# The last feed-forward layer as one stage: normalisation, router, dense experts and store

## Reference

```python
x = x + tanh(g_ffn[3]) * ffn(layernorm(x))
# ffn, H = 128, E = 16 experts of width 64, one shared expert of width 128
shared = (silu(x @ shared_gate_w) * (x @ shared_up_w)) @ shared_down_w
probs = softmax(x @ router_w)
topk_probs, topk_idx = top_k(probs, 2)
coeff = einsum('tk,tke->te', topk_probs, one_hot(topk_idx, E))
for e in range(E):
    routed += (silu(x @ gate_w[e]) * (x @ up_w[e])) @ down_w[e] * coeff[:, e]
return routed + shared
```

## Time and profile before

| what | us |
|---|---|
| median of three executions (2179.49 to 2183.73) | 2183.63 |
| the profiled execution | 2188.82 |
| its span | 2187.1 |
| last addition of the last attention ends | 2037.7 |
| normalisation ends | 2049.6 |
| router's logits on DVE | 2058.5 |
| last addition of the experts ends | 2181.4 |
| span ends, after the store | 2187.1 |

### The profile page before, as it was taken

How to read it: one execution, slowest core, us unless ns; L and a number is a source line. 1 busy time by engine, 2 the same in 40 slices (tenths; PEclk the granted TensorE clock), 3 DMA queues, 4 the chain that set the end, 5 groups by cost and what they waited for, 6 DMA issues and landing times. The chain is left out here.

```text
span 2187.1 us, 56100 instructions
## 1 busy us (share of the span) xinstructions
PE 1781.5 (81%) x22264; PEld 1239.0 (57%) x22265; DVE 1377.1 (63%) x2794; ACT 1248.9 (57%) x1585; POOL 1056.0 (48%) x1000
## 2 busy tenths in 40 slices
PE   1699636999938579999999999999627749999497
PEld 1244325888826436666666666666426638888354
DVE  3767376888854366555555655654425468888598
ACT  2357324787734236777777777777325537877221
POOL 1100004555641347777777777778442335555210
PEclk9779758999959869999999999999758869999699
DMA  6401100000041110000000000000221010000000
GB/s 172 79 6 11 26 0 1 3 3 3 2 134 40 32 36 13 12 10 13 12 10 12 12 11 12 12 11 7 64 78 44 22 40 3 3 3 3 10 15 28
DMA packets 95469, 55.15 MB, mean 25 GB/s; under 512 B 43549, under 2 KB 88936, under 8 KB 95126
## 3 DMA queue, kind: packets, MB, share of 16 engines
q1 hardware_dynamic: 87028, 42.61, 8.1%
q0 software_dynamic: 3584, 6.36, 0.8%
q10 hardware_dynamic: 4610, 2.71, 0.5%
HBM read 30.16 MB, written 13.75 MB: 20 GB/s over the span
## 5 line engine op out<-in xcount | busy, mean ns | idle before, releaser
L1412 POOL TENSOR_TENSOR aw_p_lo<-aw_p,aw_p_hi 128x512 f16<-128x512 f32 x512 | 576.8, 1158 | 190.5 <-issue 168.3
L1428 DVE TENSOR_REDUCE aw_max_part<-ps 128x1 f32<-128x512 f32 x512 | 351.3, 690 | 289.4 <-PE ps L1234 284.5
L851 POOL TENSOR_TENSOR ap_p_lo<-ap_p,ap_p_hi 128x512 f16<-128x512 f32 x256 | 291.0, 1158 | 206.2 <-issue 193.2
L1364 ACT ACTIVATE aw_p<-ps 128x1024 f32<-128x1024 f32 x256 | 259.9, 1015 | 206.1 <-PE ps L1265 204.0
L1279 PE MATMUL ps<-ctx_hi_lo,aw_p_hi 128*128 128x97 f16 x2048 | 288.7, 206 | 2.5 <-POOL aw_p_lo L1412 2.5
L1281 PE MATMUL ps<-ctx_hi_lo,aw_p_hi 128*128 128x96 f16 x2048 | 287.9, 207 | 0.0
L1283 PE MATMUL ps<-ctx_hi_lo,aw_p_lo 128*128 128x97 f16 x2048 | 287.3, 204 | 0.0
L1371 ACT ACTIVATE aw_p_hi<-aw_p 128x1024 f16<-128x1024 f32 x256 | 270.6, 1057 | 8.1
L1281 PEld LDWEIGHTS ps<-ctx_hi_lo,aw_p_hi 128*128 128x128 f16 x2048 | 197.7, 97 | 25.2
L1279 PEld LDWEIGHTS ps<-ctx_hi_lo,aw_p_hi 128*128 128x128 f16 x2048 | 196.3, 96 | 12.1 <-POOL aw_p_lo L1412 4.7
L1283 PEld LDWEIGHTS ps<-ctx_hi_lo,aw_p_lo 128*128 128x128 f16 x2048 | 201.7, 98 | 0.0
(11 more groups left out here) (422 smaller groups left out, 4874.3 us busy)
## 6 DMA issues: line engine op xcount, KB each, us to landing
sf_weights_raw<-in_L_w SPq DMA_DIRECT2D x24, 256.0 KB, 4.4
slot_scratch<-at_empty_rows SPq DMA_DIRECT2D x16, 260.0 KB
sf_fetched<-slot_scratch SPq DMA_DIRECT2D x16, 260.0 KB, 2.9
sf_weights_raw<-in_L_w SPq DMA_DIRECT2D x8, 512.0 KB
x_norm<-result_scratch SPq DMA_DIRECT2D x8, 256.0 KB, 4.0
aw_queries<-aw_queries SPq DMA_DIRECT2D x32, 64.0 KB, 1.9
aw_queries<-aw_q_lo SPq DMA_DIRECT2D x32, 64.0 KB, 2.0
raw<-in_L_q SPq DMA_DIRECT2D x3, 512.0 KB, 12.7
```

The costliest lines, as they stand in the source:

```text
L851: nc.gpsimd.tensor_tensor(p_lo[:, i % 2, h, :], p[:, i % 2, h, :], p_hi[:, i % 2, h, :], ALU.subtract).then_inc(lo_done, 1)
L1364: nc.scalar.activation(p[:, n % 2, :].rearrange("p (b q) -> p b q", b=2), s, ACT.Exp, scale=1.0 / QS).then_inc(exp_done, 1)
L1412: nc.gpsimd.tensor_tensor(p_lo[:, n % 4, cols], p[:, n % 2, cols], p_hi[:, n % 4, cols], ALU.subtract).then_inc(lo_done, 1)
L1428: nc.vector.tensor_reduce(mpart[:, b % 2, k:k + 1], ps[:, max_bank(b, k), :], AX.X, ALU.max).then_inc(m_done, 1)
```

## The change

The attention of layer 3 gets three additions. SP loads all nine experts' w1 and w2 and the router's weights at its start. POOL, before its first `ap_p_lo`, fills a selection matrix `W.select` (two affine selects over 128x1024), a zeroed coefficient tile (128x2048, fp16) and a scale. From half 16 to half 33 POOL also splits one expert in two steps: at an even half it scales w2 (128x128) and takes the high half of all three parts (128x384), at the odd half the low half.

One block then does the rest. Normalisation goes by query block. The transposes, router products and the products of the shared expert are interleaved on PE. The router's chain is the same but for its end: the coefficients are made times 8, as a high and a low fp16 half in one tile, and PE turns them (`turn_comb`). The work is a list of 36 jobs: first the shared expert for the four blocks, then for each block its eight pairs. For each of the 32 pair jobs PE spreads the coefficients of the pair over the 128 hidden rows by one more 512-column matmul, and DVE multiplies silu by them before it multiplies by the second product. POOL takes the hidden tile's low half, so that the second layer is fp16 (twelve 128-column matmuls), and its results add up in one PSUM bank (YB) over the nine experts of a block. DVE adds a block to x once, and SP stores it at once.

Core of the diff (LAG is 2, JOBS the list):

```diff
-            layernorm(nc, M, 2 * n + 1, split=n > 0, plain=True)
...
-                router(nc, M, d, n)
-                expert_ffn(nc, M, d, n)
-        store(nc, M, out)
+                W = dense_weights(nc, d, ctx)
+                attention_pairs(nc, M, n, W)
+                dense_ffn(nc, M, W, out)
...
+def load_dense_weights(sp, W):
+    sp.dma_start(W.router[:], W.w_router).then_inc(W.loaded, 16)
+    sp.dma_start(W.raw[:, :, 0:2 * D], W.w1.rearrange("e p n -> p e n")).then_inc(W.loaded, 16)
+    sp.dma_start(W.raw[:, :, 2 * D:3 * D], W.w2.rearrange("e p n -> p e n")).then_inc(W.loaded, 16)
+    sp.wait_ge(W.loaded, 3 * 16)
...
+def set_up_dense_weights(nc, pool, W):
+    link = chained(pool, W.set_up)
+    link(nc.gpsimd.memset(W.scale[:], W2S))
+    link(nc.gpsimd.memset(W.select[:], 0.0))
+    link(nc.gpsimd.memset(W.comb[:], 0.0))
+    sel = W.select[:].rearrange("p e (h n) -> p e h n", h=2)
+    for k in (0, 16):
+        link(nc.gpsimd.affine_select(out=sel, in_=sel, compare_op=ALU.not_equal, fill=1.0, base=-k,
+                                     pattern=[[-2, 8], [-1, 2], [0, 64]], channel_multiplier=1))
...
+    if part == 0:
+        pool.wait_ge(W.loaded, 3 * 16)
+        nc.gpsimd.tensor_tensor(W.raw[:, e, 2 * D:], W.raw[:, e, 2 * D:], W.scale[:].to_broadcast([P, D]), ALU.mult
+                                ).then_inc(W.scaled, 1)
+        pool.wait_ge(W.scaled, e + 1)
+        nc.gpsimd.tensor_tensor(W.hi[:, e, :], W.raw[:, e, :], M.one[:].to_broadcast([P, 3 * D]), ALU.mult
+                                ).then_inc(W.hi_done, 1)
+    else:
+        pool.wait_ge(W.hi_done, e + 1)
+        nc.gpsimd.tensor_tensor(W.lo[:, e, :], W.raw[:, e, :], W.hi[:, e, :], ALU.subtract)
...
+                def produce(j):
+                    q, e = JOBS[j]
+                    if j < NQ:
+                        pe.wait_ge(xlo_done, q + 1)
+                    if j >= 2:
+                        pe.wait_ge(silu_done, j - 1)
+                    product(AB + j % 2, e, 0, q).then_inc(a_ready, 1)
+                    if j >= NQ:
+                        k = j - NQ
+                        if e == 0:
+                            pe.wait_ge(ct_done, q + 1)
+                        if k >= 2:
+                            pe.wait_ge(sc_done, k - 1)
+                        nc.tensor.matmul(ps[:, CB + k % 2, :], W.select[:, e, :], combT[:, q, :], start=True, stop=True
+                                         ).then_inc(c_ready, 1)
+                    if j >= 2:
+                        pe.wait_ge(mult_done, j - 1)
+                    product(GB + j % 2, e, 1, q).then_inc(g_ready, 1)
...
+                def results(j):
+                    q, e = JOBS[j]
+                    pe.wait_ge(lo_done, j + 1)
+                    if e == 0 and q:
+                        pe.wait_ge(x_done, q)
+                    result(q, e, j, e == 0, False).then_inc(y_job, 1)
+                    if e == NE - 1:
+                        result(q, NE, q, False, True).then_inc(y_ready, 1)
...
+                for j in range(NQ, NJ + LAG):
+                    if j < NJ:
+                        produce(j)
+                    if j in (NQ, NQ + 1):
+                        turn_comb(j - NQ + 2)
+                    if j - LAG >= NQ:
+                        results(j - LAG)
...
+                for j in range(NQ, NJ + 1):
+                    if j < NJ:
+                        gates(j)
+                    highs(j - 1)
+                    if j in (NQ, NQ + 1):
+                        comb(j - NQ + 2)
...
+                    V.tensor_tensor(sc[:, k % 2, :], ps[:, CB + k % 2, :], silu[:, j % 2, :], ALU.mult
+                                    ).then_inc(sc_done, 1)
+                    dve.wait_ge(sc_done, k + 1)
+                    dve.wait_ge(g_ready, j + 1)
+                    V.tensor_tensor(hid[:, j % 2, :], ps[:, GB + j % 2, :], sc[:, k % 2, :], ALU.mult
+                                    ).then_inc(mult_done, 1)
...
+                for j in range(NQ, NJ + LAG + 1):
+                    if j < NJ:
+                        mult(j)
+                    i = j - LAG - 1
+                    if i >= NQ and JOBS[i][1] == NE - 1:
+                        add(JOBS[i][0])
```

More of the change, by code:

```diff
@@ L55 @@
 SV, SO = 8.0, 32.0
+HS, W2S = 8.0, 16.0
 SPLITS = (("q", P, QS * 64 ** -0.5), ("k", DC, 1.0), ("v", DC, SV), ("o", P, SO))
@@ L1679, in router @@
-        w = sb("w", [P, E])
-        bias = sb("bias", [P, 1, E])
-        b2 = sb("b2", [8, D])
-        combT = sb("combT", [8, NTOK])
-        iota = sb("iota", [P, 1, E])
-        v, e, o1, o2, t = (sb(n, [P, NT, E]) for n in ("v", "e", "first", "second", "t"))
-        m, m2, i, s, r = (sb(n, [P, NT, 1]) for n in ("m", "m2", "i", "s", "r"))
-        loaded, iota_done, logits, chain = sem("loaded"), sem("iota"), sem("logits"), sem("chain")
-        shifted, exp_done, comb_done = sem("shifted"), sem("exp"), sem("comb")
@@ L1696, in _ @@
             def _(sp):
-                sp.dma_start(w[:], d[f"L{layer}_router"]).then_inc(loaded, 16)
-                if layer < 3:
-                    sp.dma_start(bias[:, 0, :], d[f"L{layer}_router_b"]).then_inc(loaded, 16)
-                if layer == 2:
-                    sp.dma_start(b2[:], d["L2_b2"]).then_inc(loaded, 16)
+                o = out.rearrange("b (t p) f -> p (b t) f", p=P)
+                for q in range(NQ):
+                    sp.wait_ge(x_done, q + 1)
+                    sp.dma_start(o[:, tiles(q), :], M.x[:, tiles(q), :]).then_inc(stored, 16)
+                sp.wait_ge(stored, 16 * NQ)
             @block.gpsimd
@@ L1707, in _ @@
                 ins.then_inc(iota_done, 1)
+                for q in range(NQ):
+                    pool.wait_ge(var, q + 1)
+                    nc.gpsimd.tensor_tensor(rstd[:, tiles(q)], ve[:, tiles(q)], M.neghalf[:, tiles(q)], ALU.pow
+                                            ).then_inc(rstd_done, 1)
+                for j in range(NJ):
+                    hi, lo = hidden(j)
+                    pool.wait_ge(hi_done, j + 1)
+                    nc.gpsimd.tensor_tensor(lo, hid[:, j % 2, :], hi, ALU.subtract).then_inc(lo_done, 1)
@@ new lines, in route, with turn_comb @@
+                def route(q):
+                    if q == 0:
+                        pe.wait_ge(xlo_done, 1)
+                    pe.wait_ge(xt_done, q + 1)
+                    for n in range(q * TQ, (q + 1) * TQ):
+                        ins = nc.tensor.matmul(ps[:, LB, n * E:(n + 1) * E], M.xt[:, n * P:(n + 1) * P], W.router[:],
+                                               start=True, stop=True)
+                    if q == NQ - 1:
+                        ins.then_inc(logits, 1)
+                def turn_comb(q):
+                    bank = YB if q == 0 else RB
+                    if q == 0:
+                        pe.wait_ge(comb_done, 1)
+                        pe.wait_ge(xlo_done, NQ)
+                    if q >= 2:
+                        pe.wait_ge(ct_done, q)
+                    for t in range(TQ):
+                        ins = nc.tensor.matmul(ps[:, bank, t * P:(t + 1) * P], W.comb[:, q * TQ + t, :], M.ident16[:],
+                                               start=True, stop=True)
+                    ins.then_inc(ct_ready, 1)
@@ new lines, in result @@
+                def result(q, e, j, first, last):
+                    hi, lo = hidden(j)
+                    for t in range(TQ):
+                        o, tok = ps[:, YB, t * D:(t + 1) * D], slice(t * P, (t + 1) * P)
+                        nc.tensor.matmul(o, hi[:, tok], W.hi[:, e, 2 * D:], start=first and t == 0, stop=False,
+                                         skip_group_check=True)
+                        nc.tensor.matmul(o, hi[:, tok], W.lo[:, e, 2 * D:], start=False, stop=False,
+                                         skip_group_check=True)
+                        ins = nc.tensor.matmul(o, lo[:, tok], W.hi[:, e, 2 * D:], start=False, stop=last,
+                                               skip_group_check=True)
+                    return ins
```

553 lines of the change are left out of this document (199 added, 354 removed).

## The result

| | before | after |
|---|---|---|
| median, us | 2182.53 (4 runs, 2179.49 to 2183.73) | 2143.87 (4 runs, 2141.70 to 2147.12) |
| profiled execution / span, us | 2188.82 / 2187.1 | 2147.12 / 2145.3 |
| ratio | | 0.9826, 95% interval 0.9809 to 0.9843 |

The change saves 38.7 us between the medians. Both profiled executions lie above their medians, so I compare stretches inside the traces.

What follows compares the result with a forecast made beforehand. DVE was taken to set the experts' pace, after 37.6 us of engines mostly taking turns. Terms from the attention's end summed to span end 2157.3, 29.8 us less than 2187.1; 2183.6 - 29.8 gave 2154 us, range 2147 to 2166.

Steps and rivals of the forecast that it cites:

- so the forecast is 2183.6 - 29.8: Whole kernel: median of three earlier runs less the 29.8 us saved from the last attention on, giving 2154 us.
- The low end of the range, 2147: Whole kernel: fastest time allowed, from the own case with logits at 2053, where the clock rises at once.
- POOL in the attention, cost 0: Last attention: POOL's added set-up and weight splits cost nothing, hidden by its idle time; bounds 0 and 25.7 us.
- Rival 1: Last attention: POOL's additions show, 7 us for a partial miss (2161), 25.7 in full (2180); chance 0.12.
- Logits after 22.4 us: Normalisation and router: logits at 2060.1, 22.4 us after the attention's end, with PE's clock at half speed throughout.
- My other bound, 2053: Normalisation and router: logits there at 2053 if PE's clock rose at once.
- Chain and coefficients, 10.0: Router's chain on DVE after the logits: 2.0 + 8.0 us, coefficients at 2070.2.
- Jobs: Experts: PE sets the pace, job period 2.17 us, three block-end waits for DVE's addition, 6.2 us in all.
- rival 3: Experts: the clock stays at the lower level, dense matmuls take 71 us more, 2225; chance 0.04.
- Results at 0.0555 against the page's 81 ns: Experts' second layer: 0.0555 us per 128-column matmul; by the skill's 81 ns the results take 11 us more, 2165.
- Rival 2: Experts: weight loads show behind short matmuls, 29 us if uncovered (2183), a third of it 2164; chance 0.04.
- Store, 3.0: Kernel's end: 3.0 us from the last addition to the end with the store by block, against 5.7 before.

Runs made afterwards that it cites:

- before, narrow tile: Kernel before with the coefficient tile 8 columns wide and an 18-column one of the last layer's own: 2184.68 us, ratio to before 0.9997.
- doubled splits: Changed kernel with each high and low half of the weights computed twice on POOL during the attention: median 2154.89 us.

## Why the prediction missed

**The step that failed** is the last one, "so the forecast is 2183.6 - 29.8", with its range. Of the 10.0 us between 2153.8 (its result) and 2143.87, 1.1 is the median of before (2182.53 this time), 1.8 the stretch (31.6 in place of 29.8), and 7.1 lie ahead of the last attention, in a term that I put at nothing. The step held everything ahead of the attention fixed and gave the range nothing for the spread of one program's executions. Three runs that agreed within 4.3 us, and a profiled fourth 5 us above their highest, were all I had, and the fourth should have warned me. The low end of the range, 2147, came from the logits' clock alone.

The 39 executions of before that were timed in all lie between 2170.42 and 2191.70, with the median at 2183.63. If the stretch is taken from each kernel's median, 1771.0 to 1775.2 us are left in twelve of the thirteen kernels (before with its 2183.63 is one), in the middle 1773.3; in the first measurement of the changed kernel it is 2143.87 - 377.65 = 1766.2, in its second 1771.3 (2149.22 less the mean of its two stretches, 377.96). So the first four runs of the changed kernel came out some 7 us shorter than this kernel's usual time, and 1773.3 + 378.0 = 2151, inside the range, is what I now expect of it. Why those four were fast, by chance or by something of that measurement, is open; the four runs of before beside them were not (2182.53, 1.1 below the 39). That it is not the SBUF addresses is shown (before, narrow tile).

**Local terms**, from the attention's end, in the order of the working; all come from the changed kernel's trace:

- *POOL in the attention, cost 0*: right. 259.23 us from POOL's first operation to the last addition, 259.08 before. Rival 1 did not come about, and the doubled splits, which cost 6.0 us, show that little room was left.
- *Logits after 22.4 us*: wrong, 17.65. I took "the slow value because the rows on either side of the gap show 0.50". The rows ahead of the gap show PE busy 4.33 of 11.9 us and those behind it only 16-column products, and the new order puts six 512-column products there. PE started them when I said (8.36 us after the attention's end, 8.2 forecast), and the clock came up just behind them, at 2039.14. So the mis-sized term is PE's work at half clock, 14.2 us with its hand-offs, which took 9.3. My other bound, 2053 or 15.3 after, was too early.
- *Chain and coefficients, 10.0*: 10.92, and 9.73 where POOL keeps away. 0.8 and 0.4 us came from POOL's subtractions beside two of the operations, a cost that stood nowhere in the working.
- *Jobs*: a period of 2.18 us (2.17 forecast), results at 0.056, three waits of 2.08 (2.07 forecast). From the coefficients to the last addition's end I had 84.1, and it was 86.4; 1.7 of the difference is the fall of the clock at one of the waits, which stood in rival 3 only as a lasting state. Coefficients turned and first products slow for 3.4 us: forecast 3.8.
- *Results at 0.0555 against the page's 81 ns*: the trace has 0.056 in 35 of the 36 groups of twelve, over 80 us and at block ends for 24 in a row, and 0.10 in the one group of the slow stretch. Between the groups stand 512-column products. The rule of the Trainium skill (TensorE: Matmul & The Clock Gate, Back-to-back issue gap) would have cost 11 us; the measurement decides against it for this mix. Rival 2 fell with it.
- *Store, 3.0*: 2.7.

Sum from the attention's end: 119.6 forecast, 117.7 measured. A gain of 4.7 at the logits and losses of 0.9 and 2.3 behind them partly cancel, so it is luck that 29.8 comes so near to 31.6. The sign was safe: a PE with some 73 us of work sets the pace where DVE needed 106.1, as the earlier trace rows said.

## What to carry to other kernels

When dense work is put into a stretch that ran at half clock, ask what clock the new order gets, and don't take it from the rows of the old one: here that moved the logits by 4.7 us against the forecast. A wait on a dense engine has two prices, its length and the slow start that may follow; here moving one addition ahead of two multiplications saved both, 8.3 us in all. When an edit's gain matches its forecast, look whether it lies in the part that the edit touches. Before giving a range for a small change in a long program, ask for the spread of several executions; compare inside the trace, between two fixed operations, where it was more than ten times smaller for one program (0.8 us against 13).

## What the runs showed of the hardware

- A DVE operation with two inputs in SBUF and a POOL operation of the same kind held each other up: 0.42 became 1.23 and 0.80 us, POOL's 1.15 became 1.39, and the two on DVE went back to 0.42 when POOL's work was moved away. The Trainium skill (SBUF — State Buffer, SBUF: two separate sides) tells of one port pair that the two engines share and that one holds for a whole instruction. By that rule the later one ends about its own full duration after the earlier, and the trace agrees within 0.14 us: 2048.80 + 0.42 is 2049.22, measured 2049.09; for POOL 2050.45 + 1.15 is 2051.60, measured 2051.47.
- The granted clock fell to half at 7 of 24 waits of 2.07 us in an otherwise dense stream, at a different one from profile to profile, at 2 of 3 of 3.9 us, and at none of nine block ends without a wait. It came back after 3.4 us, and each fall cost 1.7 us. The Trainium skill (TensorE: Matmul & The Clock Gate, A second HAM failure mode: psum-queue depth-cycling) says that frequent short idle times between groups of matmuls can make the clock go back and forth; here single waits, some 20 us apart, did it.
- The same happens unprovoked by an edit: one program had 0.50 in one execution and 1.00 in another between 122 and 134 us, with PE busy all through in the slow one, and the two were 5.4 us apart at the end of it.
